# Gate and up products of three chunk pairs in each of groups 1 to 3 by seven block products, late sparse weights loaded twice, picks spread over both stages

## The reference

```python
def attn(h):                                   # h: 2048 tokens x 512, S = 128, F = 1248
    approx_up = h @ up_w.T
    delta = h @ gate_w.T - local_point
    ...                                        # six powers of |delta| times approx_up, each @ fuse_weight.T
    ffn = silu(h @ ffn_gate_w.T) * (h @ ffn_up_w.T) @ ffn_down_w.T
    return approx_out + ffn
def sparse(x):                                 # INTER = 1792, SPARSITY = 32, RANK = 16
    inter = x @ c1_w.T @ c2_w.T
    idx = argmax of each block of 32 of inter  # 56 rows of w1 and w2t for each token
    return relu(w1[idx] . x) @ w2t[idx]
x = layernorm(x + attn(x))
x = layernorm(x + sparse(x))
```

## Time and profile before

| | us |
|---|---|
| median of 3 runs | 721.61 (721.25 to 721.93) |
| the profiled execution | 722.09, its span 720.3 |
| TensorE busy | 706.0 (98%) |
| VectorE busy | 527.8 (73%) |
| ScalarE busy | 267.3 (37%) |
| GpSimd busy | 293.3 (41%) |
| first stage of the FFN in the chain | from 109.5 to 427.5 |
| second stage | from there to 713.7 |

### The profile page before, as it was taken

How to read it: one execution, slowest core, us unless ns; L and a number is a source line. 1 busy time by engine, 2 the same in 40 slices (tenths; PEclk the granted TensorE clock), 3 DMA queues, 4 the chain that set the end, 5 groups by cost and what they waited for, 6 DMA issues and landing times.

```text
span 720.3 us, 10333 instructions
## 1 busy us (share of the span) xinstructions
PE 706.0 (98%) x3961; PEld 382.3 (53%) x3961; DVE 527.8 (73%) x983; ACT 267.3 (37%) x450; POOL 293.3 (41%) x278
## 2 busy tenths in 40 slices
PE   7999999999999999999999999999999999999996
PEld 2444444444444444444444456666666666667763
DVE  5979897796787778677787878948885778337236
ACT  1565457444812121221222224444334333443341
POOL 0452452211111161244215666897366435742330
PEclk9999999999999999999999999999999999999999
DMA  9637309401000110110000221122222101210101
GB/s 326 257 113 223 59 3 354 111 3 56 2 15 17 22 21 2 28 27 19 6 15 19 50 49 50 32 61 16 50 72 66 47 3 59 62 45 1 59 2 58
DMA packets 40833, 44.67 MB, mean 62 GB/s; under 512 B 25296, under 2 KB 33104, under 8 KB 39888
## 3 DMA queue, kind: packets, MB, share of 16 engines
q1 hardware_dynamic: 37808, 39.29, 17.8%
q0 software_dynamic: 2112, 4.19, 3.4%
q10 hardware_dynamic: 864, 0.53, 0.2%
HBM read 34.33 MB, written 4.42 MB: 54 GB/s over the span
## 4 chain that ended last, share of the span: by engine, by line
PE 73%; DVE 7%; POOL 5%; issue 2%; ACT 1%; DMA 0%; POOLq 0%; DVEq 0%; ACTq 0%
PE acc L542 27%; PE pb L522 14%; PE pa L522 13%; PE pb L776 7%; PE pa L776 6%; PE acc L619 2%; PE acc L865 1%; DVE big L1703 1%; POOL work L1123 1%; PE pick_a L685 1%; PE pick_b L685 1%; POOL quad L1177 1%; DVE small L1592 1%; POOL big L1130 1%; DVE big L1701 1%
## 5 line engine op out<-in xcount | busy, mean ns | idle before, releaser
L542 PE MATMUL acc<-big,work 128*128 128x512 f16 x1038 | 235.1, 379 | 1.5 <-POOL work L1123 1.5
L1123 POOL TENSOR_TENSOR work<-work 128x512 f16<-128x512 f32 x92 | 110.4, 1212 | 274.7 <-ACT work L1009 214.7
L542 PEld LDWEIGHTS acc<-big,work 128*128 128x128 f16 x1038 | 101.4, 98 | 117.4 <-POOL work L1123 2.0
L522 PE MATMUL pa<-xs,big 128*128 128x512 f16 x480 | 111.2, 379 | 0.0
L522 PE MATMUL pb<-xs,big 128*128 128x512 f16 x480 | 110.1, 379 | 0.0
L1834 DVE TENSOR_TENSOR pa<-pa,big 128x512 f32<-128x512 f32 x28 | 19.6, 699 | 83.3 <-ACT big L1089 69.0
L522 PEld LDWEIGHTS pa<-xs,big 128*128 128x128 f16 x480 | 46.1, 98 | 54.0
L522 PEld LDWEIGHTS pb<-xs,big 128*128 128x128 f16 x480 | 46.1, 98 | 53.3
L619 PE MATMUL acc<-big 128*128 128x512 f16 x336 | 73.9, 379 | 0.3 <-DVE big L1439 0.2
L1009 ACT ACTIVATE work<-work 128x512 f16<-128x512 f32 x40 | 25.2, 630 | 111.5 <-DVE work L1576 111.5
L1130 POOL TENSOR_TENSOR big<-work,big 128x512 f16<-128x512 f32 x27 | 37.0, 1387 | 65.6 <-ACT big L947 65.3
(11 more groups left out here) (219 smaller groups left out, 984.5 us busy)
## 6 DMA issues: line engine op xcount, KB each, us to landing
big<-in_w_all SPq DMA_DIRECT2D x2, 3840.0 KB, 17.0
big<-in_x_t SPq DMA_DIRECT2D x16, 256.0 KB, 8.6
rows<-in_x POOLq DMA_DIRECT2D x4, 1024.0 KB, 12.7
big<-spread_rows SPq DMA_DIRECT2D x16, 256.0 KB, 6.0
big<-in_w_all SPq DMA_DIRECT2D x2, 1536.0 KB, 11.3
big<-spread_rows SPq DMA_DIRECT2D x16, 192.0 KB, 4.9
out<-rows SPq DMA_DIRECT2D x3, 1024.0 KB, 4.4
big<-in_w_all SPq DMA_DIRECT2D x1, 2048.0 KB, 14.5
```

Source lines behind the costliest of these rows:

```text
L522: mm = nc.tensor.matmul(dst[:, :], weights(wp)(kc * P, P), x_part16(g, xp, kc), start=(kc == 0 and wp == xp), stop=(kc == KC - 1 and wp == 1))
L542: mm = nc.tensor.matmul(acc[t][:, :], act_part(pair, j, ap, t * P, P), weights(wp)(0, H), start=(first and ap == wp), stop=(last and ap == 1))
L1123: nc.gpsimd.tensor_tensor(act_part(pair, j, 1), act32[j], act_part(pair, j, 0), ALU.subtract).then_inc(act_lo, 1)
```

## The change

1. In the pairs (1,1), (1,2) and (g,0), (g,1), (g,2) for g = 2, 3, gate and up are made by seven block products each (`FAST_UNITS`, eight pairs, 16 block sets). Both chunks' gates go into `pa` and `pb`, are summed and take the silu; then both ups.
2. The block sums for it are new jobs: "v" of the weights (pair u, gate or up), "y" of the x of a group. A pair can now have a second job, raised at its end and lowered in the next (`SECOND_JOB`).
3. Only sparse chunks 0 to 5 are split in group 0. Chunks 6 to 13 are loaded for their maximum, the sums v and y use their place, and they are loaded again (`load_again`) and split in (3,3), (3,4) and in unit 3 of the second stage.
4. In the first stage 8 tiles have their scores, tile 8 its z; the other 8 have theirs in the second stage, three banks in one unit and the fourth in a later one. The moments of group g-1 stand in pair (g,1) behind the first half; x1 of tile 0 is split behind the whole of pair (1,1).

```diff
-JOB_IN_SWIGLU = {9: 0, 12: 1, 14: 2, 17: 3, 18: 4, 19: 5}
+FAST = 3
+FAST_UNITS = tuple((g, u) for g in range(1, GROUPS) for u in range(FAST) if (g, u) != (1, 0))
+TILE_AT = {(1, 2): 0, (1, 3): 1, (1, 4): 2, (2, 2): 3, (2, 3): 4, (2, 4): 5, (3, 2): 6, (3, 3): 7, (3, 4): 8}
+SUM_JOBS = (("v", 1, 0), ("v", 1, 1), ("y", 1, 0), ("y", 1, 1), ("v", 2, 0), ("v", 2, 1), ("v", 0, 0), ("v", 0, 1),
...
+FIRST_JOB = {2: 0, 3: 1, 4: 3, 5: 5, 6: 6, 7: 7, 8: 8, 9: 9, 11: 11, 12: 12, 13: 13, 14: 14, 17: 15, 18: 16, 19: 17}
+SECOND_JOB = {3: 2, 4: 4, 9: 10}
+PICKS_AT = {2: 8, 4: 9, 6: 10, 9: 11, 11: 12, 13: 13, 16: 14, 18: 15}
...
+            sp.wait_ge(p34_ready, B0)
+            sp.wait_ge(pb_summed, B0)
+            load_again(0)
+            load_again(1)
...
+                half(0, z_product(tile, tile // TPG, tile % TPG, pick_a) if tile is not None else None)
+                if early is not None:
+                    scores(early, 2, pick_a)
+                    scores(early, 3, pick_b)
+                down(g, u, kind, [0])
+                half(1)
+                if tile is not None:
+                    scores(tile, 0, pick_a)
+                    scores(tile, 1, pick_b)
+                down(g, u, kind, [1])
...
+            def fast_swiglu(g, u, tile):
+
+                pair, n, b = g * U1 + u, g * C1 + u * 2, fast_block(g, u, 0)
+                take_products(b)
+                act.wait_ge(act_lo, n)
+                act.wait_ge(pa_summed, b + 1)
+                act.activation(outer(work32[:, 0:2 * GT]), halves(pa[:, :]), ACT.Silu, scale=gate_out[:, g:g + 1]).then_inc(silu_ready, 1)
+                act.wait_ge(pb_summed, b + 1)
+                act.activation(work32[:, HT:3 * HT], pb[:, :], ACT.Silu, scale=gate_out[:, g:g + 1]).then_inc(silu_ready, 1)
+                if pair - 1 in SECOND_JOB:
+                    sums_high(SECOND_JOB[pair - 1])
+                if tile:
+                    x1_high(tile)
+                take_products(b + 1)
+                if pair in FIRST_JOB:
+                    sums_high(FIRST_JOB[pair])
+                act.wait_ge(swiglu_ready, n + 2)
+                for j in range(2):
+                    act.activation(act_part(pair, j, 0), act32[j], ACT.Copy).then_inc(act_hi, 1)
+                if tile == 0:
+                    x1_high(tile)
...
-            for u in range(1, GROUPS * U1):
-                low(u, 0, u * 2)
-                if u in JOB_IN_SWIGLU:
-                    raise_quad(JOB_IN_SWIGLU[u])
-                    lower_quad(JOB_IN_SWIGLU[u])
-                low(u, 1, u * 2 + 1)
+            for n in range(1, GROUPS * U1):
+                g, u = n // U1, n % U1
+                if fast(g, u):
+                    add_products(fast_block(g, u, 0))
+                if n - 1 in SECOND_JOB:
+                    lower_quad(SECOND_JOB[n - 1])
+                if fast(g, u):
+                    if n in FIRST_JOB:
+                        raise_quad(FIRST_JOB[n])
+                    add_products(fast_block(g, u, 1))
+                    if n in FIRST_JOB:
+                        lower_quad(FIRST_JOB[n])
+                    low(n, 0, n * 2)
+                    low(n, 1, n * 2 + 1)
+                    continue
+                low(n, 0, n * 2)
+                if n in FIRST_JOB:
+                    raise_quad(FIRST_JOB[n])
+                    lower_quad(FIRST_JOB[n])
+                low(n, 1, n * 2 + 1)
+                if n in SECOND_JOB:
+                    raise_quad(SECOND_JOB[n])
...
+                if u == 1:
+                    moments(g - 1, 1)
+                    normalise(g - 1, x1_ready, middle=lambda: fast_swiglu(g, u))
+                    if g == 1:
+                        x1_low(0)
+                else:
+                    fast_swiglu(g, u)
```

More of the change, by code:

```diff
@@ L708, in unit1, with down @@
                     split_product(pb, lambda part: w1_part(s, 1, part), g).then_inc(up_ready, 1)
-                    if tile is not None and j == 1:
-                        scores(tile, 2, pick_a)
-            def down(g, u, kind, scored=None):
+                    if early is not None and j == 0:
+                        scores(early, 3, pick_b)
+            def down(g, u, kind, js=range(2)):
                 before = g * U1 + u - 1
-                for j in range(2):
+                for j in js:
                     m = before * 2 + j
@@ new lines, in unit @@
+            def unit(g, u):
+                early, tile = TILE_AT.get(unit_before(g, u)), TILE_AT.get((g, u))
+                kind = "last" if u == 0 else "first" if u == 1 else "middle"
+                if fast(g, u):
+                    fast_unit(g, u, kind, early, tile)
+                    return
+                unit1(g, u, early, tile)
+                down(g, u, kind, [0])
+                if tile is not None and tile < IN_SWIGLU:
+                    scores(tile, 0, pick_a)
+                    scores(tile, 1, pick_b)
+                down(g, u, kind, [1])
@@ L751, in _, with second2 @@
             down(1, 0, "last")
[L752 to L759 removed]
+            for n in range(U1 + 1, GROUPS * U1):
+                unit(n // U1, n % U1)
+            def second2(g, u, kind, after):
                 before = g * U2 + u - 1
@@ L768, in second2, with hidden_products @@
                                    halved=(g == GROUPS - 1 and kind != "last"))
[L769 to L780 removed]
+                    after(j)
+            def hidden_products(g, u):
                 n = g * U2 + u
[L783 removed]
                 def w_block(c, half):
@@ L1076, in take_products @@
[L1076 to L1089 removed]
+            swiglu(1, 0)
@@ L1631, in normalise @@
                                     ALU.subtract, ALU.mult).then_inc(signal, 1)
-                    if t == 1 and low is not None:
-                        x1_low(low)
+                    if t == 1 and middle is not None:
+                        middle()
                     if t == 1 and mask is not None:
```

560 lines of the change are left out of this document (339 added, 221 removed).

## The result

The changed kernel takes 754.6 us (median of 6 runs, 753.8 to 758.0), the kernel before 721.7: ratio 1.046, interval 1.044 to 1.048. The forecast was 739.0 with a range up to 746. The direction and most of the places were right; the loss is 33 us where 17.5 were expected. The execution that was profiled took 755.7, its span is 753.9.

A forecast was written before the change was run, and what follows sets the result against it. The prediction took TensorE's matmul stream as the bound. Fewer streamed columns (-9.6 us) and the added terms A to G summed to +17.5 us on the earlier median of 721.6, giving 739, range 727 to 746.

The forecast's parts named there:

- A: Group 0: GpSimd's serial chain of block sums delays the first pa copy of pair (1,1); +10.8 us, bounds 8 and 13.
- B: Pair (1,2): tile 0's x1, normalised and split after the fast pair (1,1), comes late; +7.3 us, bounds 4 and 9.
- C: Middle of pair (2,0): job 10, raised ahead of the first add_products, makes TensorE wait; +2.3 us, bounds 0 and 3.5.
- D: Fast pairs (2,1) and (3,1): moments behind the first half delay later products; 0.6 each, +1.2 us, bounds 0 and 3.
- E: End of group 3: sums, weight splits and picks delay the second stage's first pa copy; +3.0 us, bounds -1.4 and 6.
- F: Second stage: VectorE's extra picks, z, x1_low and masks make it late in places; +1.0 us, bounds 0 and 8.
- G: TensorE's clock drops in the gaps of A and B and stays low for a while; +1.5 us, bounds 0 and 4.
- the helpers keep up: Rival: the helper engines cause almost no wait, so only the -9.6 us of stream counts; 712 us, chance 0.04.
- a hidden A: Rival: group 0's chain A costs nothing while B still does; 725 to 728 us, chance 0.09.
- a smaller A: Rival: A costs only 5 to 7 us, as raises without VectorE beside them are faster; 732 to 734, chance 0.17.
- The clock that stays low: Rival: after the gaps the clock stays low, G at its upper bound of 4, helpers unchanged; 742 us, chance 0.10.
- VectorE overloaded in the second stage: Rival: F at its upper end, with a wait in each group behind moments; 746 us, chance 0.12.

The follow-up runs named there:

- the kernel with small sums: The changed kernel with the six block sums of group 0 each raised by one small GpSimd operation instead of six or seven large ones; 738.1 us.
- moving x1: The jobs later version with ScalarE's and VectorE's splits of tile 0's x1 placed earlier in pair (1,1); 749.1 us.
- The experiment with the scores: The changed kernel with the first two score products of a plain pair behind both halves of its down product instead of between them; 755.4 us.
- the filled kernel: The changed kernel with matmuls that nobody reads put ahead of what were meant as TensorE's four longest waits; 756.7 us.
- jobs later: The changed kernel with jobs 4 and 5 (weight sums read only by pair (1,2)) one pair later, and following jobs later where room is; 751.7 us.
- added additions: The kernel before the change with six 256-column GpSimd additions that nobody reads behind each low part of pairs 4 to 7; 732.6 us.

## Why the prediction was wrong

Each term by the traces: waits with their 0.16, less what stood at the place before.

| term | forecast | measured | from |
|---|---|---|---|
| stream, eight fast pairs | -9.6 | -9.6 | 14.35 a pair |
| A, first copy of (1,1) | +10.8 | +14.9 | 215.04 - 200.11 |
| B, x1 of tile 0 in (1,2) | +7.3 | +9.1 | 238.09 - (215.04 + 13.9) |
| C, middle of (2,0) | +2.3 | +2.3 | 2.1 + 0.16 |
| D, moments in (2,1), (3,1) | +1.2 | +0.6 | 0.43 + 0.16 |
| turned z in (g,3), (g,4), groups 1 and 2 | 0 | +4.2 | four waits, 3.6 |
| E, end of group 3 | +3.0 | +6.8 | five waits, 7.5, less 1.4 |
| F, second stage | +1.0 | +2.5 | three waits, 3.8, less 1.5 |
| G, clock | +1.5 | +1.5 | 238.09 to 242.53 |

The 13.9 in B is TensorE's own work between the two, from the kernel with small sums (200.11 to 214.6, less a wait of 0.6). The sum is 32.3, and 32.1 with a first stage that starts 0.2 earlier; the spans differ by 33.6. 1.5 us are not assigned. The places and the sizes are those of one execution of each kernel.

**The step that failed first is the durations in A**, and with them other terms in which GpSimd and VectorE work at once. I noted that the 6.3 of a raise "was taken while VectorE was in picks, so I use 6.0 and 5.7", and treated the two engines as independent otherwise. They are not. The five raises took 6.06, 6.26, 7.35, 6.96 and 5.60, 32.2 in place of 29.4 (28.3 without VectorE's splits); the low parts 7.0 in place of 6.4; and the first was 0.8 late: 4.2 in all, which is A's error (10.8 to 14.9). Without VectorE's splits A was 9.5, near its forecast and inside its bounds. I put the splits on no path at all, though at 1.41 us instead of 0.79 they held the gated product of (0,4). The Trainium skill (SBUF — State Buffer, the section on SBUF's two separate sides) describes this: VectorE and GpSimd share one pair of ports, given to one of them for a whole instruction, and an operation of VectorE with two inputs in SBUF takes it when GpSimd's reads SBUF too. The trace agrees that both engines lose, in the 1.05 and 0.72 of the same addition and the 6.74 and 6.85 side by side. It does not show that one stands still for the whole of the other: six splits (4.44 alone) and six additions (4.8 alone) took 6.9 together, not 9.2. It was to be looked up for a change that adds GpSimd work beside such operations.

A is a quarter of the miss. The turned z (4.2, put at nothing) and E (3.8 too small) weigh as much, then B (1.8) and F (1.5).

**B** had the right chain, as moving x1 showed. One link was longer, by B's whole error: two rows of the normalisation, 1.00 in the kernel with small sums, took 2.82. GpSimd was lowering job 6 beside them (225.94 to 228.39), and VectorE's next operation began at 228.59:

```profile
225.85 2.82 DVE L1838 TENSOR_SCALAR rows<-rows,small 128x512 f32<-128x512 f32 x2
...
228.59 0.69 DVE L1981 TENSOR_TENSOR pa<-pa,big 128x512 f32<-128x512 f32 x1
```

**The turned z** was missing from my list of waits. Its cover is 5.0 us, as in the kernel before (there an up and a gate product, now an up product and one down half), for VectorE's five small operations and a transfer. The five operations took 1.1 us before (232.68 to 233.78) and take 2.4 now (262.83 to 265.22), the same in each of the five pairs with such a wait; GpSimd raises a sum beside them:

```profile
261.97 2.40 POOL L1360 TENSOR_TENSOR quad<-xs 128x512 f32<-128x512 f16 x2
263.28 1.13 DVE L1893 TENSOR_TENSOR big<-big 128x16 f32<-128x16 f32 x1
```

The same operation in the kernel before, with GpSimd idle:

```profile
216.64 0.18 DVE L1685 TENSOR_TENSOR big<-big 128x16 f32<-128x16 f32 x1
```

The 1.3 more is enough for the waits of 1.2 and 0.6 in groups 1 and 2. So by these rows this term too comes from the work side by side; that is argued from them, and no run isolates it. The experiment with the scores shows why it could not simply be won back by order: the picks behind it are as late. **E** had its chain (splits, picks, last copy) named, but not the z behind the spread load, and four splits took VectorE 4.3 to 5.9, where my chain had it 0.7 behind ScalarE's 2.5. **F** likewise: 1.39 a split in unit 3.

**G** has the right size by luck. I took two stretches at 2 us each and a middle value; the clock fell four times, for 5.8 us of slower matmuls in all, and filling showed that three of the four cost nothing, because TensorE afterwards waits for helpers in any case. In other executions it fell at other places, in the filled kernel where it did cost 1.6. **C** and **D** had their chains; C had its size too, D was 0.6 too large.

Of the rivals, the one that the helpers keep up is refuted by 36 us of waits, a hidden A and a smaller A by 14.9 (by its own terms the smaller A would have been 733 to 735, not 732 to 734). The clock that stays low is not what made the difference: it counts for 1.5. VectorE overloaded in the second stage was half right: it is overloaded from the end of group 3 on. No version beats the kernel before; the nearest, without fast pairs in group 1 and with tile 7's z first (728.2), is some 6 us slower: its stream is 7.2 shorter, and the waits from group 2 on cost more than that.

## What to carry to other kernels

Work moved from a bound engine to an idle one is not free by that engine's idle share. Here GpSimd work that nobody waited for cost 10.8 us through VectorE. Lay it beside what VectorE does at the same time, small operations in a serial chain too, and take durations from a stretch in which both were busy, or measure one by adding operations that nobody reads. And where a saving is the sum of many small ones, count each place at which the new order asks for something within 3 us of its being made: in this kernel many of these became waits, and moving one often moved the wait to the next helper.

## What the runs showed of the hardware

- VectorE's split of 512 columns (f32 and f16 in, f16 out, all in SBUF): 0.74 us beside an idle GpSimd (4.44 for 6), 1.12 beside additions of 256 columns (6.74 for 6), 1.41 beside raises (8.46 for 6). An addition of 256 columns on GpSimd: 0.72 alone, 1.05 to 1.14 beside these splits. An addition of 16 columns on VectorE: 0.18 alone, 1.13 beside a raise. VectorE's gated products, with one input in PSUM, took 0.73 to 0.75 before, in the changed kernel and with the added additions.
- The granted clock fell to 0.50 at no fixed point of a wait. In the changed kernel it fell some 0.2 us after TensorE had resumed at 190.31 (a wait of 3.3), and at 214.4, still in the wait of 4.7. With jobs later it fell at 189.0, 2 us into a wait of 3.2; in the filled kernel at 196.9, 1.3 after the end of a wait of 2.6. Behind the same wait of 2.9 in unit 4 it fell in the filled kernel and not in the changed one. It stayed low for 3.4 us in most places, 6.8 in the kernel with small sums (218.1 to 224.9) and 10.2 with x1 earlier (225.0 to 235.2). Twelve matmuls of 512 columns took 4.45 us in such a stretch, 2.75 outside.
- A turned z issued behind SyncE's load of spread winners (399.07) could be used 5.3 us after its issue, against 2.3 when it went first (398.59).
